# A four-block transformer kernel on one core: VectorE makes the low part of queries and keys instead of GpSimd

## The reference

```python
for block in (0, 1, 2, 3):
    mod = silu(c) @ ada_w + ada_b               # shift, scale and gate, twice
    h = modulate(norm(x), ...)                  # block 0: rmsnorm, the others: layernorm
    q, k, v = split(h @ qkv_w + qkv_b)          # block 0 also normalises q and k by head
    o = softmax(q @ k.T * 9 ** -0.5) @ v        # blocks 0 to 2: over the 128 tokens of a sequence
    x = x + gate * (o @ proj_w + proj_b)        # block 3: over the 16 heads of a token
    x = x + gate2 * mlp(modulate(norm(x), ...)) # gelu between two linear layers
```

## Time and profile before

| what | value |
|---|---|
| median of 3 runs | 1560.69 us (1559.18 to 1561.07) |
| time of the profiled execution | 1559.51 us |
| span of the profiled execution | 1557.7 us, mean granted TensorE clock 0.921 |
| busy: PE | 1299.0 us (83%) |
| busy: DVE | 1105.1 us (71%) |
| busy: ACT | 964.3 us (62%) |
| busy: POOL | 320.9 us (21%) |

### The profile page before, as it was taken

How to read it: one execution, slowest core, us unless ns; L and a number is a source line. 1 busy time by engine, 2 the same in 40 slices (tenths; PEclk the granted TensorE clock), 3 DMA queues, 4 the chain that set the end, 5 groups by cost and what they waited for, 6 DMA issues and landing times.

```text
span 1557.7 us, 36854 instructions
## 1 busy us (share of the span) xinstructions
PE 1299.0 (83%) x13314; PEld 833.1 (53%) x13314; DVE 1105.1 (71%) x2807; ACT 964.3 (62%) x2139; POOL 320.9 (21%) x446
## 2 busy tenths in 40 slices
PE   6365778888869999999999999999787888878887
PEld 4111434554446666666666666666555555555654
DVE  3755666777668888888888888888676567675452
ACT  0032555556536677777777767777577667777673
POOL 2010011111111221211221112211232333323201
PEclk9975787899878999999999999999988898999898
DMA  6213444224414445555555444444996799989500
GB/s 186 85 30 72 107 109 109 70 56 116 109 54 117 117 118 132 129 130 129 129 136 134 123 120 125 117 117 121 73 124 124 89 120 69 131 133 125 66 26 23
DMA packets 198481, 163.63 MB, mean 105 GB/s; under 512 B 80136, under 2 KB 182480, under 8 KB 192160
## 3 DMA queue, kind: packets, MB, share of 16 engines
q1 hardware_dynamic: 189920, 153.60, 50.3%
q10 hardware_dynamic: 8384, 7.69, 1.7%
HBM read 98.05 MB, written 62.41 MB: 103 GB/s over the span
## 4 chain that ended last, share of the span: by engine, by line
PE 50%; ACT 17%; DVE 13%; issue 11%; ACTq 3%; DMA 3%; SPq 1%; DVEq 0%; POOL 0%; POOLq 0%
PE lin L1496 10%; PE lin L1480 9%; PE o_bank L1433 6%; PE score_bank L1327 4%; ACT p_room L729 4%; ACT hT_last L710 3%; PE score_bank L1371 3%; DVE maxima L1116 3%; PE st_bank L1402 3%; ACT h2T L715 2%; PE lin L1484 2%; ACT stack_room L800 2%; PE score_bank L1343 2%; PE score_bank L1337 2%; ACT h1T L715 1%
## 5 line engine op out<-in xcount | busy, mean ns | idle before, releaser
L1116 DVE TENSOR_REDUCE maxima<-score_bank 128x4 f32<-128x512 f32 x512 | 329.1, 684 | 147.4 <-PE score_bank L1371 145.0
L729 ACT ACTIVATE p_room<-st_bank 128x512 f32<-128x512 f32 x512 | 278.6, 604 | 136.6 <-PE st_bank L1402 91.3
L1496 PE MATMUL lin<-w_f,gelu 128*128 128x144 f32 (+1 forms) x1280 | 194.0, 312 | 18.4 <-ACT max_T L812 17.6
L613 POOL TENSOR_TENSOR part_low<-qk_rest,part_mid 96x512 bf16<-96x512 f32 x96 | 113.9, 1187 | 414.6 <-DVE part_mid L1099 414.6
L1371 PE MATMUL score_bank<-stack_room 62*128 62x128 bf16 x2048 | 107.9, 228 | 109.2 <-ACT stack_room L800 39.2
L1496 PEld LDWEIGHTS lin<-w_f,gelu 128*128 128x128 f32 (+1 forms) x1280 | 182.6, 211 | 26.9 <-ACT max_T L812 25.2
L1480 PE MATMUL lin<-h2T,w_h 128*128 128x512 f32 (+1 forms) x320 | 170.0, 630 | 9.6 <-ACT gelu L845 6.3
L1433 PE MATMUL o_bank<-p_room,v_room 128*32 128x128 f32 x4096 | 173.6, 290 | 0.0
L1371 PEld LDWEIGHTS score_bank<-stack_room 62*128 62x128 bf16 x2048 | 62.5, 98 | 183.7 <-issue 46.2
L604 POOL TENSOR_TENSOR x<-x,gated 128x288 f32<-128x288 f32 x64 | 52.4, 819 | 466.1 <-DVE gated L1164 466.1
L845 ACT ACTIVATE gelu<-lin 128x512 f32<-128x512 f32 (+1 forms) x160 | 91.0, 588 | 78.6 <-PE lin L1484 77.8
(11 more groups left out here) (193 smaller groups left out, 2412.8 us busy)
## 6 DMA issues: line engine op xcount, KB each, us to landing
stack_room<-stack_dram SPq DMA_DIRECT2D x96, 512.0 KB, 8.2
stack_dram<-part_high SPq DMA_DIRECT2D x64, 288.0 KB, 3.9
gates<-gates_dram SPq DMA_DIRECT2D x64, 288.0 KB, 4.1
norm_room<-stack_dram SPq DMA_DIRECT2D x32, 512.0 KB, 8.7
stack_dram<-part_mid SPq DMA_DIRECT2D x64, 192.0 KB, 3.2
stack_dram<-part_high SPq DMA_DIRECT2D x64, 144.0 KB, 3.9
stack_dram<-part_mid SPq DMA_DIRECT2D x64, 96.0 KB, 3.1
stack_dram<-part_low SPq DMA_DIRECT2D x64, 96.0 KB, 2.2
```

What stands on the lines that cost most here:

```text
L613: eng.tensor_tensor(part_low[:, T, :], qk_rest[:, T, :], part_mid[:, T, :], ALU.subtract)\
L729: eng.activation(probs[:, i % PBUFS, :], st_bank[i % 2][:, :], ACT.Exp, scale=float(HD) ** -0.5)\
L1116: eng.tensor_reduce(maxima[:, b, CH * c:CH * c + CH], bank_of(f"S{i}")[:, :].rearrange("p (h k) -> p h k", h=CH), AX_X, ALU.max)\
L1496: ins = eng.matmul(o, gelu[0:k, T, b * TOK:(b + 1) * TOK], w_f2[l][0:k, T, :], start=T == 0, stop=T == FCT - 1)
```

## The change

`low` leaves GpSimd's program, with its five places in the body. VectorE's `mid` gets the same subtraction right behind the cast, behind a wait for the cast's own semaphore. Waits of others for `qk_low` stay, and VectorE now signals it.

```diff
@@ gpsimd
-            def low(L, T):
-
-                if not ok(L):
-                    return
-                need(eng, "qk_mid", L, T)
-                if T == 0:
-                    need(eng, "parts_stored", L - 1, LAST_STORE)
-                eng.tensor_tensor(part_low[:, T, :], qk_rest[:, T, :], part_mid[:, T, :], ALU.subtract)\
-                   .then_inc(S["qk_low"], 1)
-
             def body(g):
                 J, L, M, P, Q = g + 1, g + 2, g + 3, g - 1, g - 2
-                if not normed_heads(L):
-                    low(L, 1)
-                    low(L, 2)
                 mods_of(P, 1)
                 mods_of(M, 0)
                 order_keys(J, 0)
@@
                 order_keys(J, 3)
                 add_mlp(Q, 1)
-                if normed_heads(L):
-                    for T in range(QKT):
-                        low(L, T)
-                if not normed_heads(M):
-                    low(M, 0)
@@ vector, in mid(L, T)
                 eng.tensor_copy(part_mid[:, T, :], qk_rest[:, T, :]).then_inc(S["qk_mid"], 1)
+                need(eng, "qk_mid", L, T)
+                eng.tensor_tensor(part_low[:, T, :], qk_rest[:, T, :], part_mid[:, T, :], ALU.subtract)\
+                   .then_inc(S["qk_low"], 1)
```

## The result

The changed kernel takes 1578.47 us (median of 4 runs, 1569.59 to 1581.8) against 1559.93 us for the kernel before (4 runs, 1557.27 to 1561.07): a ratio of 1.0112, with a 95% interval of 1.0069 to 1.0156. In a later comparison it took 1572.19 us (6 runs) against 1557.94, a ratio of 1.0085 (1.0057 to 1.0114). So it is about 1% slower. The profiled execution took 1577.44 us.

A forecast was written before the change was run, and what follows sets the result against it. VectorE's order was taken to bound normed bodies, TensorE blocks 1 and 2. Terms 8.9 + 4.0 + 2.1, with 0.1 for block 3's tiles 0, gave 15.1 us: 1574.6 us profiled, 1575.8 as median, 1.0% slower; range 1568 to 1582.

The forecast's parts named there:

- block 0's term: Normed bodies: 1.29 us later in each of six, 0.58 in each of two outer ones; 8.9 us together.
- block 3's: Seven bodies of block 3: GpSimd's copies start earlier and delay `last_parts`, 0.3 us each; 2.1 us, bounds 0 and 4.2.
- the term of blocks 1 and 2: Sixteen bodies, each 0.25 us longer, nearly all from tile 1; 4.0 us, at the upper end 6.1.
- the 0.73: Upper-end gap in us from a low's start to VectorE's next op, instead of 0.60; total 20.0 us, not 15.1.
- Tile 0: Blocks 1 and 2: the low is paid by the add no longer stretched; the reciprocal starts 0.01 us later.
- the wait for `o_tok`: Blocks 1 and 2, tile 1: `divide`'s output comes 0.60 us later, of which TensorE sees 0.24 us.
- Rival 2: Normed bodies: longer TensorE pauses keep the clock at 1.2 GHz longer, 5 us lost, 1581 us; chance 0.10.
- no change: Whole kernel: two errors cancel, time within 1557.6 to 1563.8 us; chance 0.05.
- a faster kernel: VectorE's low runs at the cast's 0.42 us, not 0.69, giving 1557 us; chance 0.05.
- rival 1: All lows are seen, TensorE's gaps in tiles 1 and 2 being no slack: 1588 us; chance 0.12.
- Rival 3: Mostly hidden: stores and ScalarE bind all eight normed bodies, ScalarE stays last at tile 1; 1565 us; chance 0.13.
- the stretches: VectorE ops lengthened beside GpSimd's lows: adds by 0.70 us, normed bodies' second cast by 0.84; both go away.

The follow-up runs named there:

- order held: Changed kernel, but GpSimd waits at the head of its body for tile 2's low, so its copies stay where they were: 1572.73 us, again 1570.01 us.
- the timed pair: The changed kernel, and the same with GpSimd's mods and keys copies held back, timed on one chip: 1572.19 against 1570.01 us.
- keys first: Kernel before, lows still on GpSimd, but its mods and `order_keys(J, 0)` ahead of `low(L, 2)` outside block 0: 1559.05 us, ratio 1.0002.
- GpSimd's lows later: Kernel before, all lows on GpSimd, but most at its body's end wait until VectorE has passed `divide(g, 2)`: 1541.25 us, ratio 0.9878.
- VectorE's lows later: Changed kernel with VectorE's lows moved to where it waits anyway, GpSimd waiting at its head for tile 2's cast: 1537.92 us, ratio 0.9865.

## Why the forecast held, and where its terms were off

The forecast was 1.0% slower. It was measured at 1.12% and 0.85%, and both intervals hold 1.0%. That the total comes so near owes something to luck. In the profiles block 0's term came out smaller than forecast (6.2 and 7.8 us for 8.9) and block 3's larger (8.1 and 5.6 for 2.2), and the two errors cancel in part. Only the term of blocks 1 and 2 was right in size as well as in kind.

**The price of one low.** 0.69 us, a start 0.45 to 0.46 after the cast, and the next op, where it did not wait for anything, 0.60 to 0.62 after the low (353.80 to 354.41, 741.49 to 742.10). So the 0.60 of the earlier trace rows was the right row to take, and the 0.73 of the earlier trace rows did not carry over. The prediction names two prices for the 0.73, 3.9 us and 3 to 5; by its own terms it is 20.0 - 15.1 = 4.9. The reading by the Trainium skill (VectorE: DVE Perf Modes, "Two Vector instructions with no wait between them"), that the longer gap belongs to an op which begins in another block of partitions, came out as it said.

**Normed bodies.** From the first cast to TensorE's scores it was 354.23 - 348.82 = 5.41 us and is 360.09 - 353.34 = 6.75: +1.34 against +1.29. The pauses of TensorE in the six bodies, 4.64, 4.60, 3.95, 4.20, 5.06 and 4.27 us, became 5.97, 5.92, 5.30, 5.76, 6.49 and 6.34, each 1.3 to 2.1 longer. Where bodies repeat evenly, their casts of tile 0 stood 53.0 us apart before and stand 54.3 apart now. So the mechanism and its size per body were right. What did not hold is that it adds up over all eight bodies: block 0 as a whole grew by 6.2, 7.8, 6.0, 8.5 and 6.8 us in the five profiles that have VectorE's low in it, where the forecast said 8.9. In each of the five, one body became shorter by 1.2 us in spite of its longer pause (here the one from 247.24 to 299.02 us, 51.78 instead of 53.01; in three of the others the one ahead of it); which work caught up there, no run settles.

**Blocks 1 and 2.** 3.7 us in four profiles (627.89 to 628.20 against 624.30) where the forecast said 4.0. Tile 0 cost 0.02 (forecast 0.01). The body grew by 0.215 us, 3.66 / 17 (17 bodies lie between the two cuts, the forecast counted 16), against 0.25. Tile 1 alone does this. From TensorE's line 1453 (now 1438) at tile 1 to its next wait for `maxima`, with tile 2 in between, it is 19.37 us before (736.44 to 755.81) and 19.31 now (744.39 to 763.70); what grows, from 17.36 to 17.62, is the stretch from there to tile 1 of the next body. Tile 2 stayed hidden. The forecast had only the wait for `o_tok`; a wait of 0.22 us for the bank that `maxima` frees (742.93) came beside it, by the same 0.60 us. `o_tok` is ready at 744.33, and TensorE takes it 0.06 later, but the timeline names `v_room` in its place, which ended at 744.35; before it waited for `h2T`. In the kernel before, the same matmul began at 736.44 while `v_room` was still being written until 736.63, so `v_room` is hardly what it waits for. In one of these bodies (929.16) `o_tok` is named, as the forecast had it.

**Block 3.** The mechanism was as forecast: copies of `order_keys` fell into `last_parts`. The profile shows stretched ops there in six of the seven bodies: three subtractions of 2.67 to 2.68 us, one cast of 4.41, and two pairs of shorter ones. VectorE's busy time grew by 52.3 us where the forecast had 66 - 23 = 43; with the order held it is 1143.1 us instead of 1157.4, so these stretches account for the difference. The op that took 2.67 us began 0.08 before the pair of copies and ended 0.55 after it, so both copies hit it; the forecast had taken half of the delay that this gives. The Trainium skill (SBUF — State Buffer, "SBUF: two separate sides") says that such ops of VectorE and GpSimd lock each other out for a whole instruction, and the trace agrees: when the subtraction was recorded to begin (1317.07), GpSimd was already in a small copy of `mods_of` (1317.03 to 1317.21), the two large copies followed without a gap, and VectorE was let in only behind them. But the size of the term, 2.1 us with bounds 0 and 4.2, can't be confirmed: 8.1 and 5.6 us in two profiles of the changed kernel, 2.2 us between the timed pair, and nothing measurable in keys first, which has such collisions in the kernel before. This is the term that the forecast can't claim: that the copies collide is shown, what that costs is not.

**The clock.** Rival 2 said that longer pauses of TensorE would cost clock and add some 5 us of work. TensorE's busy time in block 0 fell from 273.25 to 269.59 us at a granted clock of 0.80 against 0.81. Over all profiles it is 269.3 to 273.5 us in the three with block 0's program of before and 267.3 to 271.6 in the five with VectorE's low in it. No added work shows, so this rival falls. The rivals of no change and of a faster kernel are outside the interval, and so is rival 1 at 1.7%, which had already taken only half of what tiles without any slack would cost. Rival 3, mostly hidden (0.3%), is outside it too.

**What the forecast looked at without drawing the conclusion.** It counted the stretches as a gain of the change: 0.70 us in each add and 0.84 in a normed body's cast. By its own figures that is 24 x 0.70 + 8 x 0.84 = 23.5 us, more than the loss of 15.1. Starting GpSimd's lows later, which takes most of them away and adds nothing to VectorE, gains 19 us. The change spends them all on an op put right behind the cast, where TensorE waits for what follows. "GpSimd's work costs nothing as work" was right, and its 0% in the chain of waits said so; what it cost stood in that chain under VectorE's name.

## What to carry to other kernels

The place of an instruction cost more here than the engine that runs it: the same 96 lows gave +1% right behind the cast, and -1.2 to -1.35% in the gaps where VectorE waits or, for most of those at the end of a body, on GpSimd 1.4 to 5.5 us later (715.28 instead of 0.50 after the cast at 713.41; 348.21 instead of 0.50 after the one at 342.25). Before moving work from a helper engine, compare the longest with the median duration of the ops that run beside it (1158 against 459 ns here): a stretched op on the path can be had back by starting the helper's work later. And ask what was queued behind the work that moves, since it will start earlier, beside other neighbours.

## What was not expected of the hardware

- Beside one GpSimd low of 1.16 us a cast of 0.42 us took 1.26 and an add of 0.46 took 1.16. Beside two copies, 2.04 us together, a subtraction of 0.69 us took 2.67: 1.98 more. There the GpSimd ops became longer by 0.4 us at most (the low beside the cast took 1.53 us, a single copy in the changed kernel up to 1.27), so the VectorE op paid nearly all. It isn't always so: with keys first, the subtraction at 737.52 took 0.72 us, hardly more than normal, and GpSimd's small copy at 737.60 beside it took 0.69 instead of 0.19.
- A shorter pause of TensorE sometimes kept its clock, for a moment. With GpSimd's lows later, the pause of 3.28 us before 346.82 was followed by eight score matmuls in 0.40 us at a granted clock of 1.00 (2.4 GHz), where after 5.06 us they had taken 0.61 at 0.50 (1.2 GHz). But the clock fell to 0.50 just behind them, at 347.9, and stayed there until 351.3; before the change it was at 0.50 from 352.5 to 359.3. It was no rule: with VectorE's lows later a pause of 3.08 us was followed by 0.61, and before the change one of 4.60 by 0.40. TensorE's busy time in block 0, for the same instructions, was 273.25, 269.59, 266.09 and 274.84 us (before, changed, and the two faster kernels), at granted clocks of 0.81, 0.80, 0.82 and 0.80. Profiles of one and the same block 0 program differ by up to 4.3 us in it, so this order says nothing about the four kernels.
- The pause of 5.06 us became 3.28 with GpSimd's lows later, 1.78 less, while the cast accounts for 0.84. VectorE also stood some 0.95 us further ahead of TensorE at the start of the chain (it began 2.01 us before TensorE's last matmul ended, against 1.06). What brought it ahead stays open.
